# The last two batches of a fused attention and FFN layer: residual, transposes, bias and stores in another order

## The reference

```python
def attn(x, wq, wk, wv, wo):
    q = (x @ wq.T).reshape(b, t, 16, 128).transpose(0, 2, 1, 3)
    ...
    scores = jnp.einsum('bhtd,bhsd->bhts', q, k_full) / np.sqrt(HEAD_DIM)
    attn = _masked_softmax(scores, mask)      # k <= q and (k < 4 or k >= q - 31)
    out = jnp.einsum('bhts,bhsd->bhtd', attn, v_full)
    return out.transpose(0, 2, 1, 3).reshape(b, t, 2048) @ wo.T

def ffn(x, weight, bias):
    w_scale = max(|weight|, axis=1) / 127; w_q = round(weight / w_scale)
    x_scale = max(|x|, axis=2) / 127;      x_q = round(x / x_scale)
    return (x_q @ w_q.T) * x_scale * w_scale + bias

x = x + attn(_layernorm(x), ...)
x = x + ffn(_layernorm(x), ...)
```

## Time and profile before

| | us |
|---|---|
| median of 3 runs | 634.55 |
| lowest and highest | 634.49, 634.63 |
| time of the profiled execution | 634.63 |
| span of the profiled execution | 632.8 |
| PE busy | 599.3 (95%) |
| DVE busy | 544.8 (86%) |
| ACT busy | 399.7 (63%) |
| POOL busy | 307.8 (49%) |

### The profile page before, as it was taken

How to read it: one execution, slowest core, us unless ns; L and a number is a source line. 1 busy time by engine, 2 the same in 40 slices (tenths; PEclk the granted TensorE clock), 3 DMA queues, 4 the chain that set the end, 5 groups by cost and what they waited for, 6 DMA issues and landing times.

```text
span 632.8 us, 18148 instructions
## 1 busy us (share of the span) xinstructions
PE 599.3 (95%) x7589; PEld 529.5 (84%) x7589; DVE 544.8 (86%) x1084; ACT 399.7 (63%) x631; POOL 307.8 (49%) x302
## 2 busy tenths in 40 slices
PE   5759999999999999999999999999999999999983
PEld 4547888889898988989898888989898888989872
DVE  5876899989898988989898998989898998988885
ACT  5676766566666666666666666667666666665740
POOL 1142445464565546455554646456554745535440
PEclk9989999999999999999999999999999999999996
DMA  9931401213040311203040221304030120304000
GB/s 295 352 103 20 116 1 49 55 35 85 3 117 2 86 34 46 73 15 105 1 120 2 67 52 37 83 9 112 3 96 24 53 68 20 99 1 118 3 18 34
DMA packets 33841, 41.31 MB, mean 65 GB/s; under 512 B 3936, under 2 KB 24416, under 8 KB 33760
## 3 DMA queue, kind: packets, MB, share of 16 engines
q1 hardware_dynamic: 33616, 40.02, 22.9%
q10 hardware_dynamic: 144, 0.13, 0.1%
HBM read 10.26 MB, written 4.19 MB: 23 GB/s over the span
## 4 chain that ended last, share of the span: by engine, by line
PE 87%; DVE 7%; ACT 3%; issue 1%; POOL 1%; DMA 1%; POOLq 0%; SPq 0%; ACTq 0%
PE ps L551 26%; PE ps L429 25%; PE ps L456 7%; PE ps L396 7%; PE ps L405 6%; PE ps L512 5%; PE ps L533 4%; PE ps L534 4%; PE ps L384 1%; PE ps L578 1%; DVE WoT L1008 1%; DVE Qs L892 1%; PE ps L566 1%; PE ps L336 1%; DMA X<-in_L_attn_x 1%
## 5 line engine op out<-in xcount | busy, mean ns | idle before, releaser
L429 PE MATMUL ps<-xT,WqT 128*128 128x256 f16 x1536 | 178.2, 273 | 2.0 <-DVE WqT L1008 1.3
L551 PE MATMUL ps<-WoT,pool 128*128 128x256 f16 x1536 | 178.0, 273 | 0.2 <-DVE pool L916 0.2
L429 PEld LDWEIGHTS ps<-xT,WqT 128*128 128x128 f16 x1536 | 147.0, 98 | 19.1 <-issue 3.0
L551 PEld LDWEIGHTS ps<-WoT,pool 128*128 128x128 f16 x1536 | 147.5, 98 | 16.4 <-DVE pool L916 0.3
L1203 POOL TENSOR_TENSOR small<-E,rr 128x576 f32<-128x576 f32 x63 | 72.6, 1152 | 99.8 <-DVE rr L911 99.8
L775 ACT ACTIVATE pool<-ps 128x512 f16<-128x512 f32 x128 | 69.5, 595 | 81.7 <-PE ps L534 81.6
L1209 POOL TENSOR_TENSOR PP<-small,PP 128x576 f16<-128x576 f32 x63 | 80.9, 1284 | 68.2 <-ACT PP L768 68.2
L735 ACT ACTIVATE Qs<-ps 128x576 f16<-128x576 f32 x128 | 82.4, 644 | 43.6 <-PE ps L429 43.6
L1195 POOL TENSOR_TENSOR Sm<-Sm,mx 128x576 f32<-128x576 f32 x64 | 73.7, 1152 | 54.2 <-DVE mx L902 52.9
L892 DVE TENSOR_TENSOR Qs<-ps,Qs 128x576 f16<-128x576 f32 x128 | 92.6, 724 | 3.2 <-ACT Qs L735 3.0
L916 DVE SCALAR_TENSOR_TENSOR pool<-ps,pool 128x512 f16<-128x512 f32 x128 | 81.8, 680 | 0.8 <-ACT pool L775 0.8
(11 more groups left out here) (110 smaller groups left out, 888.0 us busy)
## 6 DMA issues: line engine op xcount, KB each, us to landing
VW<-Vn SPq DMA_DIRECT2D x48, 120.0 KB
big<-Vn SPq DMA_DIRECT2D x48, 120.0 KB
X<-in_L_attn_x SPq DMA_DIRECT2D x16, 256.0 KB, 7.7
VW<-VW SPq DMA_DIRECT2D x16, 256.0 KB, 3.2
big<-big SPq DMA_DIRECT2D x16, 256.0 KB, 3.4
out<-pool SPq DMA_DIRECT2D x15, 256.0 KB, 3.6
big<-in_L_attn_wq SPq DMA_DIRECT2D x4, 512.0 KB, 7.6
pool<-in_L_attn_wo SPq DMA_DIRECT2D x4, 512.0 KB, 9.1
```

The source lines that it names most:

```text
L429: a = pe.matmul(banks[BANK_Q[f]][:, j * 256:j * 256 + 256], WqT[:, k, wl, h * 128:h * 128 + 128], xT[:, b % 2, k, xl, :], start=(n == 1), ...
L551: a = pe.matmul(banks[BANK_OUT][:, t * 256:t * 256 + 256], OT[:, p, ol, h, t * 128:t * 128 + 128], WoT[:, 4 * g + h, wl, :], start=first, ...
```

## The change

Only the written-out end is touched, and no operation is added to or taken from the arithmetic.

- DVE: `ffn_residual(14)` stands behind `s_max(63)`, where it stood ahead of `q_low(63, 0)`.
- DVE: `ffn_quant(14)` stands ahead of the two `o_low(63)`, where it stood behind them. `with_bias(14)` stands behind `ffn_quant(15)`, where it stood ahead of `ffn_residual(15)`.
- PE: `ffn_t(14)` stands between `out_proj(62)` and `out_proj(63)`, where it stood behind both.
- SP and ACT: the last two batches are stored as four halves, all from SP, each when its half is done; the store from ACT is gone.

```diff
@@ SP @@
             store(B - 3)
-
-            sp.wait_ge(f_z, 2)
-            sp.dma_start(out_v[B - 2], yo[:, B % 2]).then_inc(out[B % 2], 16)
-            sp.wait_ge(f_z, 3)
-            sp.dma_start(out_v[B - 1][:, 0, :], yo[:, (B - 1) % 2, 0, :]).then_inc(out[(B - 1) % 2], 16)
-            sp.wait_ge(out[0], 16 * (B // 2))
+            for b in (B - 2, B - 1):
+                for t in range(2):
+                    sp.wait_ge(f_z, 2 * (b - B + 2) + t + 1)
+                    sp.dma_start(out_v[b][:, t, :], yo[:, b % 2, t, :]).then_inc(out[b % 2], 16)
+            sp.wait_ge(out[0], 16 * (B // 2 + 1))
             sp.wait_ge(out[1], 16 * (B // 2 + 1))
@@ PE @@
             out_proj(u)
+            ffn_t(B - 2)
             out_proj(u + 1)
-            ffn_t(B - 2)
             ffn_mm(B - 2)
@@ ACT @@
             ffn_t_evac(B - 1)
-            act.wait_ge(f_z, 4)
-            act.dma_start(out_v[B - 1][:, 1, :], yo[:, (B - 1) % 2, 1, :]).then_inc(out[(B - 1) % 2], 16)
@@ DVE @@
             o_low(u - 2, 1)
-            ffn_residual(B - 2)
             q_low(u + 1, 0)
             q_low(u + 1, 1)
             probs(u)
             s_max(u + 1)
+            ffn_residual(B - 2)
             ffn_stats(B - 2)
@@ DVE @@
             ffn_norm(B - 2)
+            ffn_quant(B - 2)
             o_low(u + 1, 0)
             o_low(u + 1, 1)
-            ffn_quant(B - 2)
-            with_bias(B - 2)
             ffn_residual(B - 1)
             ffn_stats(B - 1)
             with_bias(B - 1)
             ffn_norm(B - 1)
             ffn_quant(B - 1)
+            with_bias(B - 2)
             ffn_out(B - 2)
```

## The result

The changed kernel takes **638.24 us** (636.25 to 639.77) against 634.59 us: a ratio of 1.0054, 95% interval 1.0036 to 1.0073. It is slower, by 3.65 us, and it scatters more than the kernel before. Its fifteen single executions in this measurement lie in three groups: 636.2, 636.25; then 637.56 to 638.43; then 638.98 to 639.79. Those of the kernel before, in this and the later comparisons, lie between 633.85 and 634.98, with ten of 55 at 635.6 to 636.8. I forecast 636.6, with a range of 635.9 to 638.0; the median is outside.

The account below looks back on a forecast made before the run. PE was taken to bound the kernel until the last projection, then a 12.9 us chain that nothing overtakes. The steps, 1.75 + 0.22 + 0.08 = +2.05 us, on the 634.55 us median gave 636.6 us; range 635.9 to 638.0.

Parts of the forecast that it names:

- Step 1: Residual of batch 14 behind s_max(63) on DVE: out_proj(60) waits 2.5 us, of which +1.75 us remains (bounds 1.3 to 2.5).
- The gain in front of q_low(63): On DVE, taking the residual out ahead of q_low(63) brings only its first half forward; gain on the path 0.
- Step 2: Four transposes before out_proj(63) on PE delay its end by +0.22 us (bounds 0.2 to 0.4); DVE's moved quantisation costs 0.
- Step 3: with_bias(14) in DVE's window before ffn_out(14): cover used up, +0.05 to +0.1 us, taken as 0.08.
- Step 4: Four 128 KB stores on SP at the end: no queue backs up, 0 us, bounds -0.1 to +0.3.
- rival B: The clock falls in the new gap before out_proj(60): 0.9 to 1.7 us more, 637.5 to 638.3 us; chance 0.18.

## Why the prediction was wrong

**Step 1, the wait.** Right in place and size. out_proj(60) waited 2.39 us for the residual (forecast 2.5), and of this 1.69 us arrived at out_proj(61) (forecast 1.75), with p_transpose(62) 3.96 after out_proj(60) (forecast 3.97). The gain in front of q_low(63) was nothing, as worked out.

**Step 2, the transposes.** +0.22, exactly the row it was taken from, and no wait for o_low(63).

**Step 3, the bias.** +0.21 and not 0.08. The step's failing term is the handover: an instruction that waits on the one right ahead of it on DVE started 0.15 us after its end here, where I put in 0.06, and the same again between the end of ffn_out(14) and ffn_out(15), 0.1.

**Step 4, the stores.** Nothing seen: the changed kernel's four stores land in 1.7 us each, and with the residual back, the stores and all else together are not told from no change.

The sum with the measured terms is 1.69 + 0.22 + 0.21 = 2.12 us, 636.7 from 634.59. The profiles of the kernel with its gap filled give 2.08, its times 636.82 and 636.41, and the two executions of the changed kernel with the clock kept took 636.2. So the sum was sound, **for an execution that keeps its clock**. The step that failed is the choice between the forecast and rival B: the sum let everything behind the gap run at full pace, 3.97 us from out_proj(60) to p_transpose(62). It was 3.96 with the clock kept, and 5.40, 5.63 and 6.62 in the three profiles of the changed kernel. I gave the falling clock a chance of 0.18; in this measurement 13 of 15 executions were over 637.5, and the three profiles all show the fall. My ground against it was that no gap under 2 us had lowered the clock in one trace. That said little about a gap of 2.39 that comes 1 us of idle time and 0.8 us of matmuls after another, and it was not even true of the kernel in general: two profiles, of the changed kernel with the residual back and of the kernel before with only the transposes moved, show a fall just behind the wait of 1.6 us.

Rival B's price was mis-sized too. I gave 0.9 to 1.7 us on top of 636.6. Measured on the distance between the two projections it was 1.44 and 1.67 in the middle group, within that, but 2.66 in the slow one, since the clock stayed down for the whole of the next projection, 5.1 us. I had priced the fall by the three to four us of half pace behind the one long gap of the trace, as if that were the most that could happen. But there the clock was down from about 42.9 to 49.7 (worked out from the 0.72 and 0.58), and PE stood idle for the first 3.2 us of that. In the slow execution it was idle for only 1.3 us of a fall about as long, and so more work ran at half pace. The median of the changed kernel, 638.24, is rival B's.

The Trainium skill (TensorE: Matmul & The Clock Gate, "Why this matters for your kernels") warns of idle gaps between bursts of matmuls, after which the clock is back at its lower level, but it gives this for gaps longer than the one here. The profile after shows what it says of the long ones, at a shorter one: idle for 2.39 us, granted clock 0.79 and 0.50 in the stretches that hold the gap and what follows. The measurement decides: in this kernel a gap of that length was not safe.

## What to carry to other kernels

Before an instruction is moved behind others on an engine, list who waits for its semaphore elsewhere: here one 0.74 us residual, moved by 5 us on an engine with time to spare, held up the head of the busiest engine's queue. A new wait on TensorE costs its own length less what later waits absorb, and in addition a stretch at half pace that comes in some executions and not in others, so a gap like those of this kernel should be priced with both. How often the fall comes sets the median: it came in 13 of 15 executions at 2.4 us, which is a median with the fall, and in a minority at 1.6 us in the kernel before. Such gaps were worth filling here, with work that is ready or even with matmuls for nothing; of whether this holds in a kernel that is less dense on PE no run speaks.

## What the runs showed of the hardware

- The granted clock fell at gaps much shorter than the 4.76 us gap of the kernel before: at one of 2.39 us in three profiles of four that have it unfilled, and at one of 1.6 us in two profiles.
- The fall need not lie inside the gap. At 1.6 us it came some 0.9 us after PE was busy again, and in one of the three profiles at 2.39 us about 0.1 us after (moments worked out from the mean clocks of the stretches).
- The same program has different times for this reason, in steps: 635.9, 637.7 and 639.5 us with one moved instruction. With the wait of 1.6 us filled by other work, six executions lie between 632.18 and 632.78.
- Once fallen, the clock stayed down for different times after the same gap: until between 606 and 608 in one execution, until between 608 and 610 in another, 2.5 us longer measured from scores(63). The time lost was about half of what PE worked meanwhile.
- Matmuls for nothing made a kernel faster twice, by the medians: by 1.4 us in a gap of 2.4 us, and by 0.5 us at the end.
